# Int4 feed-forward net: every integer weight block multiplied unscaled, its scale applied as the sum is read from PSUM

## What is computed

```python
def _L1_ffn_ref(x, gate_q, gate_s, up_q, up_s, down_q, down_s):   # H = 512, I = 1792, G = 128
    def dequant(q, s, g=G):          # q: [out, in] in [-8, 7]; s: [out, in//g]
        O, In = q.shape
        return (q.reshape(O, In // g, g).astype(s.dtype) * s[:, :, None]).reshape(O, In)
    Wg, Wu, Wd = dequant(gate_q, gate_s), dequant(up_q, up_s), dequant(down_q, down_s)
    gate_score = jax.nn.silu(jnp.einsum('bsh,ih->bsi', x, Wg))
    intermediate = gate_score * jnp.einsum('bsh,ih->bsi', x, Wu)
    return jnp.einsum('bsi,hi->bsh', intermediate, Wd)
```

## Time and profile before

| | |
|---|---|
| median of 3 runs | 680.3 us (680.12 to 681.38) |
| profiled execution, span from first to last instruction | 678.2 us |
| TensorE busy | 667.4 us, 98% |
| VectorE, ScalarE, GpSimd busy | 420.0 (62%), 318.2 (47%), 167.4 us (25%) |
| granted clock of TensorE, mean | 0.995 |
| first matmul of the last net, last VectorE instruction of it | 499.8, 675.7 us |

### The profile page before, as it was taken

How to read it: one execution, slowest core, us unless ns; L and a number is a source line. 1 busy time by engine, 2 the same in 40 slices (tenths; PEclk the granted TensorE clock), 3 DMA queues, 4 the chain that set the end, 5 groups by cost and what they waited for, 6 DMA issues and landing times.

```text
span 678.2 us, 9098 instructions
## 1 busy us (share of the span) xinstructions
PE 667.4 (98%) x3040; PEld 550.7 (81%) x3040; DVE 420.0 (62%) x596; ACT 318.2 (47%) x497; POOL 167.4 (25%) x177
## 2 busy tenths in 40 slices
PE   8979999999999999999999999999999999999997
PEld 6858888888788888888888888888888888888885
DVE  5875674444656443444453434453679998899997
ACT  5885725245543232232222322222558885588851
POOL 4640020000000400000000000000017778877774
PEclk9979999999999999999999999999999999999999
DMA  8510022101011212310211010101132222222222
GB/s 251 148 58 24 24 87 76 62 10 34 18 39 63 87 38 86 127 54 28 62 35 59 31 58 29 56 16 31 58 98 83 86 70 75 78 79 92 86 72 94
DMA packets 22234, 45.13 MB, mean 67 GB/s; under 512 B 6469, under 2 KB 10309, under 8 KB 22149
## 3 DMA queue, kind: packets, MB, share of 16 engines
q1 hardware_dynamic: 20148, 41.44, 19.7%
q0 software_dynamic: 2048, 3.22, 1.9%
HBM read 42.54 MB, written 2.10 MB: 66 GB/s over the span
## 4 chain that ended last, share of the span: by engine, by line
PE 92%; ACT 3%; SPq 2%; issue 1%; DMA 1%; DVE 1%; DVEq 0%; ACTq 0%
PE ps_up L1206 9%; PE ps_up L1205 9%; PE ps_up L1207 9%; PE ps_down L1205 8%; PE ps_down L1206 8%; PE ps_down L1207 8%; PE ps_gate L1205 7%; PE ps_gate L1206 6%; PE ps_gate L1207 6%; PE ps_m L1320 3%; PE ps_m L1321 3%; PE ps_gate L1320 3%; PE ps_gate L1321 3%; PE ps_down L1320 2%; PE ps_down L1321 2%; PE ps_m L1241 2%
## 5 line engine op out<-in xcount | busy, mean ns | idle before, releaser
L628 ACT ACTIVATE w_hi<-w_raw 128x1024 fp32r<-128x1024 f32 (+5 forms) x66 | 51.0, 772 | 84.7 <-DVE w_raw L907 63.3
L696 ACT ACTIVATE act_hi<-gated 128x512 fp32r<-128x512 f32 (+2 forms) x50 | 31.5, 632 | 123.0 <-DVE gated L995 123.0
L561 POOL TENSOR_TENSOR w_lo<-w_raw,w_hi 128x256 fp32r<-128x256 f32 x22 | 21.7, 987 | 259.2 <-ACT w_hi L628 259.2
L1205 PE MATMUL ps_down<-act_hi,w_hi 128*128 128x512 f32 (+1 forms) x212 | 83.2, 392 | 0.0
L1207 PE MATMUL ps_down<-act_hi,w_lo 128*128 128x512 f32 (+1 forms) x212 | 82.6, 390 | 0.0
L1206 PE MATMUL ps_down<-act_lo,w_hi 128*128 128x512 f32 (+1 forms) x212 | 82.6, 390 | 0.0
L1205 PE MATMUL ps_up<-h_hi,w_hi 128*128 128x512 f32 (+1 forms) x208 | 81.2, 390 | 0.0
L1206 PE MATMUL ps_up<-h_lo,w_hi 128*128 128x512 f32 (+1 forms) x208 | 81.2, 390 | 0.0
L1207 PE MATMUL ps_up<-h_hi,w_lo 128*128 128x512 f32 (+1 forms) x208 | 80.9, 389 | 0.0
L995 DVE TENSOR_TENSOR gated<-gated,ps_up 128x512 f32<-128x512 f32 (+1 forms) x48 | 32.9, 686 | 76.9 <-PE ps_up L1207 53.8
L1205 PE MATMUL ps_gate<-h_hi,w_hi 128*128 128x512 f32 (+1 forms) x192 | 77.4, 403 | 1.7 <-ACT gated L686 1.3
(11 more groups left out here) (176 smaller groups left out, 1411.2 us busy)
## 6 DMA issues: line engine op xcount, KB each, us to landing
w_raw<-in_ffn_gu SPq DMA_DIRECT2D x28, 512.0 KB, 3.5
w_raw<-in_ffn_dn SPq DMA_DIRECT2D x16, 448.0 KB, 3.3
w_raw<-in_cond_gu SPq DMA_DIRECT2D x9, 512.0 KB, 3.5
xp<-in_x SPq DMA_DIRECT2D x8, 256.0 KB, 5.5
xp<-in_x SPq DMA_DIRECT2D x1, 2048.0 KB, 10.8
out_t<-xp SPq DMA_DIRECT2D x8, 256.0 KB, 2.0
s_bc<-in_ffn_up_s SPq DMA_DIRECT2D x14, 128.0 KB, 3.1
w_raw<-in_cond_dn_a SPq DMA_DIRECT2D x4, 384.0 KB, 3.2
```

Source lines behind the costliest of these rows:

```text
L561: nc.gpsimd.tensor_tensor(w_lo[:, s, n], w_raw[:, s, n], w_hi[:, s, n].bitcast(F32), ALU.subtract).then_inc(w_ready, 1)
L628: nc.scalar.activation(w_hi[:, s, n], w_raw[:, s, n], ACT.Copy).then_inc(w_hi_done, 1)
L696: nc.scalar.activation(act_hi[0:m, ds(2 * i + jj, 1), chunk(c)].rearrange("p a n -> p (a n)"), gated[0:m, c, :], ACT.Copy).then_inc(act_hi ...
L1205: nc.tensor.matmul(ps[0:m, :], w_hi[0:r, s, cols], rhs_hi(k, r), start=start and n == 0, stop=False)
```

## The change

All blocks of the last net are integers now and none is scaled before its matmuls. The last net leaves the list of phases. In its place stands a list of groups, one for each weight block (`plan_groups`), 168 in all, on which every engine's order and counts rest. A group is one block against all 1024 tokens, four matmuls, in one of four PSUM buffers of 1024 columns (two banks each), taken in turn. A letter says who reads it: `a` ScalarE, `v` VectorE, `h` half each. TensorE may start a group once the group four before is read.

GpSimd loses the low parts of the weights and gets the up sums' join, the product of the second half of each unit, the low part of each unit in one pass of 1024, and three sums for each down block. VectorE multiplies the first half of a unit. Scales come once, by four transfers ahead of cond1's weights. The weights, 1024 or 896 columns of integers, land in `w_int` (two slots) and are converted by ScalarE to `w_q` (three slots). Loops are written out.

```diff
+Group = namedtuple("Group", "n name k by m ea ev")
+def plan_groups():
+    gate_up = [("g", 0, "a"), ("g", 1, "v"), ("u", 0, "a"), ("u", 1, "v"), ("g", 2, "v"), ("u", 2, "a"), ("u", 3, "v"), ("g", 3, "v")]
+    down = ["a", "v", "a", "v", "h", "v", "v"]
...
+            for o, ks in ((0, range(6)), (1, range(6)), (0, (6,)), (1, (6,)), (2, range(7)), (3, range(7))):
...
-        group_banks = [ps_gate[0][:, :], ps_gate[1][:, :], ps_m[:, 0:CT], ps_m[:, CT:WT], ps_up[0][:, :], ps_up[1][:, :]]
+        group_banks = [ps_gates, ps_m, ps_downs, ps_ups]
...
 # SP, ahead of cond1's weights
+                    sp.dma_start(s_group[:, :, :], d["ffn1_group_s"].rearrange("t p g -> p t g")).then_inc(s_in, 16)
+                    for k in range(2):
+                        sp.dma_start(s_up[:, k, :], d["ffn1_up_s"][:, k * P:(k + 1) * P].rearrange("t p -> p t"),
+                                     allow_slow_non_contiguous=True).then_inc(s_in, 16)
...
 # GpSimd
+            def unit_join(u):
+                pool.wait_ge(dve_read, group_of[part * (ACT_TILES + HK) + j, "u", 3].ev)
+                nc.gpsimd.tensor_tensor(up_sum[:, u % 2, :], up_sum[:, u % 2, :], up_more[:, u % 2, :], ALU.add).then_inc(up_done, 1)
+            def unit_product(u):
+                pool.wait_ge(gate_done, u + 1)
+                pool.wait_ge(up_done, u + 1)
+                nc.gpsimd.tensor_tensor(gate, gate, up_sum[:, u % 2, chunk(1)], ALU.mult).then_inc(half_done[1], 1)
+            def unit_lo(u):
+                pool.wait_ge(unit_hi_done, u + 1)
+                nc.gpsimd.tensor_tensor(act_lo[:, j, :], gate_sum[:, u % 2, :], act_hi[:, j, :].bitcast(F32), ALU.subtract).then_inc(unit_ready, 1)
...
 # ScalarE
+            def group_tile(n, u, begun):
+                if u > 1:
+                    act.wait_ge(unit_ready, u - 1)
+                scaled(group_of[n, "g", 0], gate_sum[:, u % 2, :])
+                if begun:
+                    unit_silu(u - 1)
+                scaled(group_of[n, "u", 0], up_sum[:, u % 2, :])
+                integers(n + 2)
+                scaled(group_of[n, "u", 2], up_more[:, u % 2, :])
+                if begun:
+                    unit_hi(u - 1)
...
 # VectorE
+            def group_tile(n, u, begun):
+                dve.wait_ge(act_read, group_of[n, "g", 0].ea)
+                added(group_of[n, "g", 1], gate).then_inc(dve_read, 1)
+                dve.wait_ge(act_read, group_of[n, "u", 0].ea)
+                added(group_of[n, "u", 1], up).then_inc(dve_read, 1)
+                if begun:
+                    unit_product(u - 1)
+                dve.wait_ge(dve_read, group_of[n, "g", 1].ev)
+                added(group_of[n, "g", 2], gate).then_inc(dve_read, 1)
+                dve.wait_ge(act_read, group_of[n, "u", 2].ea)
+                added(group_of[n, "u", 3], more).then_inc(dve_read, 1)
+                dve.wait_ge(dve_read, group_of[n, "g", 2].ev)
+                added(group_of[n, "g", 3], gate).then_inc(dve_read, 1)
...
 # TensorE
+            def group(g, hi, lo):
+                bank, col = group_bank(g), (g.k + HK * (g.name == "u")) * P
+                weights = w_q[:, g.n % 3, col:col + P]
+                for c in range(CH):
+                    nc.tensor.matmul(bank[:, chunk(c)], weights, hi[:, chunk(c)], start=True, stop=False)
+                    last = nc.tensor.matmul(bank[:, chunk(c)], weights, lo[:, chunk(c)], start=False, stop=True)
+                last.then_inc(group_ready, 1)
+            def bank_free(g):
...
+                before = groups[g.m - len(group_banks)]
+                if before.by != "v":
+                    pe.wait_ge(act_read, before.ea)
+                if before.by != "a":
+                    pe.wait_ge(dve_read, before.ev)
```

More of the change, by code:

```diff
@@ L29 @@
 ACT_TILES = 7
+NT1 = F1 // P
 UQ = 2
@@ L35 @@
 GQ = HK + UQ
-assert UQ == CH
 PACK = F1 + H
@@ L49 @@
 WARM = 12
-Phase = namedtuple("Phase", "name kind layer part tiles first t0 g0 d0 m0 q0 a0 f0 raw0 loads prep")
+Phase = namedtuple("Phase", "name kind layer part tiles first t0 g0 d0 m0 raw0 loads prep")
 def plan_phases():
@@ L68, in plan_phases @@
         ("cond1", "down", "cond1", 0, HK, 0, 1, "split"),
[L69 to L72, removed]
     ]
-    t0, g0, d0, m0, q0, a0, f0, raw0 = 0, 0, 0, 0, 0, 0, 0, [-16, 0]
+    t0, g0, d0, m0, raw0 = 0, 0, 0, 0, [-16, 0]
     phases = []
     for name, kind, layer, part, tiles, first, loads, prep in steps:
-        phases.append(Phase(name, kind, layer, part, tiles, first, t0, g0, d0, m0, q0, a0, f0, tuple(raw0), loads, prep))
+        phases.append(Phase(name, kind, layer, part, tiles, first, t0, g0, d0, m0, tuple(raw0), loads, prep))
         for j in range(tiles):
@@ L87, in plan_phases, with add @@
             m0 += tiles
[L88 to L94, removed]
-    return phases
+    return phases
+Group = namedtuple("Group", "n name k by m ea ev")
+def plan_groups():
+    gate_up = [("g", 0, "a"), ("g", 1, "v"), ("u", 0, "a"), ("u", 1, "v"), ("g", 2, "v"), ("u", 2, "a"), ("u", 3, "v"), ("g", 3, "v")]
+    down = ["a", "v", "a", "v", "h", "v", "v"]
+    groups = []
+    def add(n, name, k, by):
+        last = groups[-1] if groups else None
+        ea, ev = (last.ea, last.ev) if last else (0, 0)
+        groups.append(Group(n, name, k, by, len(groups), ea + (by in "ah"), ev + (by in "vh")))
+    for part in range(2):
+        n = part * (ACT_TILES + HK)
+        for j in range(ACT_TILES):
+            for name, k, by in gate_up:
+                add(n + j, name, k, by)
+        n += ACT_TILES
+        for o, ks in ((0, range(6)), (1, range(6)), (0, (6,)), (1, (6,)), (2, range(7)), (3, range(7))):
+            for k in ks:
+                add(n + o, "d", k, down[k])
+    return groups
 def adaln_ffn(nc, d, out):
@@ L378, in w_prod_count @@
         def w_prod_count(ph, i, jj):
-            scaled = sum(p.tiles for p in phases if p.prep == "scale")
-            if ph.prep == "scale":
-                return ph.m0 + 2 * i + jj + 1
-            return scaled + ph.t0 - named["ffn1 gate/up a"].t0 + 2 * i + jj + 1
+            return ph.m0 + 2 * i + jj + 1
         def h_seen(ph):
@@ L1032, in group_tile @@
                     if c > 0:
-                        unit_product(ph, i, jj, 0)
-                    elif not isinstance(i, int) or 2 * i + jj > 0:
-                        unit_product(ph, i, jj - 1, CH - 1)
+                        dve.wait_ge(half_added, 2 * HK)
+                    nc.vector.tensor_tensor(here[:, chunk(c)], here[:, chunk(c)], both[:, chunk(c)], ALU.add).then_inc(last_sum, 1)
             def down_tile(ph, o):
-                for c in range(0 if ph.prep == "dequant" else CH):
+                for c in range(CH):
@@ L1499, in _ @@
                         t_down(ph, c)
+            for g in groups:
+                part, j = divmod(g.n, ACT_TILES + HK)
+                if g.k == 0:
+                    pe.wait_ge(int_done, g.n + 1)
+                bank_free(g)
+                if g.name == "d":
+                    if j == ACT_TILES:
+                        pe.wait_ge(unit_ready, ACT_TILES * part + g.k + 1)
+                    group(g, act_hi[:, g.k, :], act_lo[:, g.k, :])
+                else:
+                    if g.n == 0 and g.name == "g":
+                        pe.wait_ge(h_ready, 2 * CH * HK + CH * (g.k + 1))
+                    group(g, y_hi[:, g.k, :], y_lo[:, g.k, :])
 def _lay_out(i):
```

518 lines of the change are left out of this document (203 added, 315 removed).

## The result

| | before | after |
|---|---|---|
| median of 4 runs | 680.25 us (680.12 to 681.38) | 685.25 us (683.61 to 685.89) |
| span of the profiled execution | 678.2 | 684.0 |
| last net on TensorE, first matmul to the end of the last | 499.8 to 674.1 | 500.7 to 673.2 |
| last VectorE instruction ends | 675.7 | 679.6 |

The account below looks back on a forecast made before the run. TensorE's matmuls were taken to bound the kernel before; after, 19.9 us won there would be lost to a loop of waits through GpSimd's low part. GpSimd's late end adds 2.7: 680.3 + 2.7 = 683.0 us, range 672 to 690.

Parts of the forecast that it names:

- Removed matmuls, 19.9 us: Last net on TensorE: 672 matmuls instead of 760, 88 x 0.2267 = 19.9 us less; a gate/up tile then needs 7.25.
- Wider reads: Passes at 1024 columns: ScalarE read 1.11, Silu 1.06, VectorE read 1.28, half product 0.69, GpSimd 2.41 us.
- rival (a): Cheap low part: GpSimd's 1024 columns take 1.83 us, the turn 8.06, the schedule ends at 674.3, faster; chance 0.13.
- Engine sums: Per gate/up tile: VectorE 6.6, ScalarE 5.9, GpSimd 6.1 us against TensorE's 7.25, so no engine is over.
- The ring of 8.64 us: Gate/up tiles: waits through ScalarE, VectorE and GpSimd's low part back to ScalarE's gate read take 8.64 us against 7.25.
- The total on TensorE: Last net: part a loses 10.4 us to waits and part b 9.5, together 19.9, as much as is won.
- The end: Last down blocks: GpSimd's late sums make VectorE end at 678.4 instead of 675.7, +2.7 us.
- Output transfers follow as before: After VectorE's last sum: the output transfers follow unchanged, no time added.
- Scales' transfers at nothing: Three extra SP transfers ahead of cond1's weights, 25 us of cover: taken as no cost.
- rival (d): The scales' short runs hold cond1: up to 11 us, 694; chance 0.16 together with (c).
- rival (c): VectorE's and GpSimd's half products meet: product 1.3 us, turn 9.25, 690.2 us; chance 0.16 together with (d).
- Rival (b): Last net: TensorE stays the bound, the loop closes within 7.25 us, most of 19.9 is won, 662 us; chance 0.09.

Follow-up runs that it names:

- run 7: The changed kernel (two gate buffers) with GpSimd's low part for tokens 0 to 511 alone, the other half left out; 675.1 us.
- run 1: The changed kernel with three buffers for the gate sums instead of two; 679.3 us, ratio to before 0.999.
- run 2: The changed kernel with one extra 256-column GpSimd pass per unit, between ScalarE's high part and GpSimd's low part; 694.15 us.
- run 3: The changed kernel with one extra 256-column GpSimd pass per unit, before GpSimd's join of the two up sums; 686.7 us.
- run 4: The version with three gate buffers (679.3 us) without GpSimd's half of the product, VectorE's half kept; 672.0 us.
- run 6: The version with three-slot gate and down sums and another end (672.8 us), plus one late GpSimd instruction that nobody waits for; 675.6 us.
- run 5: The changed kernel with another end alone: VectorE reads the whole last fifth group and takes over a GpSimd sum, one GpSimd sum gone; 682.1 us.
- runs 8 and 9: 8: changed kernel, three slots for gate and down sums, earlier fifth-group read, run 5's end, 672.8 us; 9: that, low part half on VectorE, 672.4 us.

## Why the prediction was right, and what it missed

**Removed matmuls, 19.9 us**: right. 3040 to 2952 instructions, and a tile that nobody holds up takes 7.25 us (the first of part b, 587.23 to 594.48).

**Wider reads**: right within 0.01 us for all of them (forecast: ScalarE 1.11 and 1.06, VectorE 1.28 and 0.69, GpSimd 2.41). GpSimd's line through 0.73, 1.29 and 2.41 us for 256, 512 and 1024 columns is straight; rival (a) falls. The Trainium skill's figure (GPSIMD Engine Reference, section 3.1), 4.5 us for 2048 columns, lies within 4% of that line continued (4.65); no run here has 2048. Run 7 shows what (a) was about: with a low part of 1.29 us, shorter even than the 1.83 of (a), the kernel is 10 us faster.

**Engine sums**: right as sums, and they decide nothing. In the last net VectorE is busy 140, GpSimd 126 and ScalarE 114 of 172.5 us.

**The ring of 8.64 us**: right. 8.55 to 8.60 measured in the eight full tiles, with the wait named, in ten. Runs 1, 2, 3 and 7 show it as cause and not as company: opened it gives 0.5 to 0.7 us a tile, lengthened by 0.73 it takes 0.69 more, and the same work outside does not touch it. The hand-over of 0.05 held (0.03 to 0.07). The total on TensorE, 20.0 us lost against 19.9, is closer than its parts: the down blocks lost 2.3 us in each part where 1.7 were priced, and the gate/up tiles lost some 1 us less than priced. That the sum fits to 0.1 is luck.

**The end**: the size was right to 0.3 us and one term was left out. VectorE ends 178.9 us after the first matmul of the last net; the forecast was 678.4 - 499.8 = 178.6. That, too, is in part luck, for three misses nearly cancel. The last low part ended 154.9 us after the first matmul and not 154.5; the last block's two sums took 4.2 us and not 3.8, the second of them 1.77 for 1.30 beside VectorE's addition, as in the earlier trace rows; and VectorE's addition after it took 0.8 with its hand-over and not 1.2. The term that failed is the sentence "Output transfers follow as before". They do, but the span does not end with them: it ended 5.2 us after GpSimd's last instruction, and that had moved from 669.9 to 678.8. It is worth 1.9 us, the largest part of what the forecast missed: the change is 5.0 us by the medians where 2.7 were forecast. The profiled span was 3.1 us over its forecast (684.0 against 678.2 + 2.7): 1.9 here, 0.3 above, and 0.9 before the last net began, which was there long before it (below). In the time 2.25 is left of that, since 1.6 us lay around the span of the profiled run, not the 2.1 taken over from the median of before, and the median run was 0.4 shorter than the profiled one. The prediction asked only who computes last, not which engine is done last.

**Scales' transfers at nothing, rival (d)**: nothing of it shows, though no run leaves them out. SP's transfers of `s_up` and ScalarE's first use of cond1's weights, after the change, which answer to the earlier trace rows:

```profile
440.27 2.65 SPq L481 DMA_DIRECT2D s_up<-in_ffn_up_s  x2
...
464.78 0.62 ACT L636 ACTIVATE w_hi<-w_raw 128x512 fp32r<-128x512 f32 x1
```

ScalarE starts on the weights 0.87 us later than before (463.91) and does not wait for them. The last net's first matmul came at 500.70 instead of 499.82, 0.88 later. But a transfer of weights far ahead of all this went out at 302.06 instead of 301.19: the 0.87 us were there before the scales were asked for. In the nine other profiles, all with the same transfers, the first matmul lies between 499.1 and 501.1.

**Port collision, rival (c)**: the mechanism is real, and its condition was not met in the changed kernel, except in the last unit of each part. GpSimd's half ended 0.5 us ahead (0.7 predicted), and 12 of 14 products ran free. With the third slot the halves met and the product took 1.01 to 1.17 in the full tiles, which is why the expected 10 us of run 1 were 6. The prediction's own rule said that it "holds if the halves meet"; the expectation of run 1 forgot to ask whether opening the ring would make them. By the Trainium skill (SBUF — State Buffer, who interferes with whom) a VectorE instruction with two SBUF inputs contends with a GpSimd instruction that reads SBUF. Runs 1 and 4 bear it out: VectorE's product takes 1.01 to 1.17 beside GpSimd's half and 0.68 without it.

**Rival (b)**, 662 us: not reached by any version. Even with both obstacles gone a third ring of 7.6 us stands (run 4): TensorE's first group, ScalarE's gate read, Silu and up read, VectorE's add, product and gate read, back to the PSUM buffer. That ring is read from the rows of run 4 (a first group at 530.99, the gate read at 532.26, VectorE's product at 536.56, its read of the buffer until 538.44, the next tile at 538.59); no run opens it.

## What to carry to other kernels

Halving the number of instructions by doubling their width changed the sums of busy time little here and lengthened a ring of waits that runs through a few of them. Before such a change, write out the ring that goes through a buffer with two slots, step by step, and compare it with the time of one tile; a third slot was the cheap cure here (6 us). After opening a ring, work out again who meets whom: the next limit can be one that the old timing kept apart by half a microsecond. And look at which engine is finished last, not only at who produces the last result.

## What the hardware showed unexpectedly

The span ended 5.2 to 5.3 us after GpSimd's last instruction in each profile in which that engine was late: 678.79 and 684.0 in the changed kernel, 672.47 and 677.7 (run 1), 687.27 and 692.5 (run 2), 680.55 and 685.8 (run 3), 666.47 and 671.7 (run 4), 668.14 and 673.4 (run 7), and with one instruction of 0.11 us added for that purpose (run 6, 669.38 and 674.6). Where GpSimd was done early, with 8.3 and 6.8 us to the end, that came 2.5 and 2.7 us after VectorE's last sum (before and run 5). In runs 8 and 9 it came 2.8 and 2.9 us after VectorE's, and 5.2 after GpSimd's as well, so these two do not tell which of them set it. What fills the 5.2 us the trace does not show; it has no records there. The Trainium skill (Runtime: NRT & Kernel Launch, the preamble/postamble breakdown) lists a closing barrier of about 1.5 us that waits for all engines, and nothing longer for GpSimd; no run here shows that barrier by itself.

VectorE's reads of PSUM with one SBUF operand (1.26 to 1.29 us at 1024 columns) were not slowed by GpSimd's passes beside them in any of these runs; only instructions of VectorE with both inputs in SBUF were.
